# Attention on one core: TensorE's order laid out anew, the maxima split on GpSimd and copied on ScalarE, value products in a burst of three and one

## What is computed

```python
qkv = (x @ Wqkv).reshape(b, t, 3, H, hd).transpose(2, 0, 3, 1, 4)
q, k, v = (qkv[0], qkv[1], qkv[2])
scores = jnp.einsum('bhqd,bhkd->bhqk', q, k) * hd ** (-0.5)
scores = jnp.where(causal, scores, -jnp.inf)
attn = jax.nn.softmax(scores, axis=-1)
out = jnp.einsum('bhqk,bhkd->bhqd', attn, v)
return out.transpose(0, 2, 1, 3).reshape(b, t, c) @ Wproj + bproj
```

## Time and profile before

| what | before |
|---|---|
| median of three runs | 268.45 us (267.53 to 268.66) |
| profiled execution, its own time | 269.36 us |
| its span, first to last instruction | 267.5 us |
| mean granted TensorE clock | 0.852 of full speed |
| busy: VectorE (DVE) | 186.9 us, 70% |
| busy: TensorE (PE) | 161.9 us, 61% |
| busy: ScalarE (ACT) | 148.7 us, 56% |
| busy: GpSimd (POOL) | 74.6 us, 28% |

### The profile page before, as it was taken

One profiled execution on the slowest core, in us unless ns is written; L12 is line 12 of the kernel. 1 busy time (PEld: TensorE's weight loads), 2 busy tenths in 40 slices (PEclk: granted clock), 3 DMA queues, 4 the chain that ended last, 5 costly groups with the idle time before them and its releaser, 6 DMA issues.

```text
span 267.5 us, 4246 instructions
## 1 busy us (share of the span) xinstructions
PE 161.9 (61%) x1515; PEld 100.7 (38%) x1519; DVE 186.9 (70%) x523; ACT 148.7 (56%) x327; POOL 74.6 (28%) x88
## 2 busy tenths in 40 slices
PE   0222136907523400731848967898998998796985
PEld 0102034606412300401733524645545544453754
DVE  0688787899996697597584578778878877623411
ACT  3455769367795526693415452455645654876431
POOL 6243612234304224296014973000000000003110
PEclk9999999965795555595777977599999999999999
DMA  6995000000000000000000340312000000000011
GB/s 184 400 430 219 1 0 0 0 0 4 0 0 1 0 0 0 0 1 0 2 0 27 98 96 20 60 40 29 2 2 4 2 4 2 3 3 1 2 39 39
DMA packets 4491, 11.50 MB, mean 43 GB/s; under 512 B 1267, under 2 KB 2644, under 8 KB 3828
## 3 DMA queue, kind: packets, MB, share of 16 engines
q1 hardware_dynamic: 3510, 10.04, 10.9%
q0 software_dynamic: 960, 1.19, 1.8%
HBM read 8.24 MB, written 0.52 MB: 33 GB/s over the span
## 4 chain that ended last, share of the span: by engine, by line
PE 39%; DVE 38%; ACT 8%; POOL 5%; issue 4%; DMA 4%; SPq 1%; DVEq 0%; ACTq 0%
DVE negmax L1201 8%; PE ps L1551 6%; PE ps L1356 5%; PE ps L1491 4%; POOL uh L445 4%; PE ps L1581 3%; PE ps L1587 3%; PE ps L1447 2%; DMA cw<-in_cond_w 2%; PE ps L1531 2%; PE ps L1438 2%; PE ps L1415 2%; DVE u L1009 2%; ACT xhat L653 2%; DVE fg L1051 2%
## 5 line engine op out<-in xcount | busy, mean ns | idle before, releaser
L1201 DVE TENSOR_REDUCE negmax<-ps 128x1 f32<-128x384 f32 (+3 forms) x96 | 52.8, 595 | 16.0 <-PE ps L1493 16.0
L743 ACT ACTIVATE PT<-ps 128x1024 f32<-128x1024 f32 x40 | 40.8, 1025 | 34.6 <-PE ps L1537 34.2
L378 POOL TENSOR_TENSOR rstd<-veps,mhalf 128x4 f32<-128x4 f32 x8 | 8.1, 1011 | 114.4 <-DVE veps L840 114.4
L1491 PE MATMUL ps<-KS,QS 48*128 48x128 bf16 (+3 forms) x128 | 33.3, 325 | 1.1 <-DVE negmax L1201 0.8
L1356 PE MATMUL ps<-k_f,u 128*128 128x128 f32 x40 | 10.0, 425 | 32.6 <-ACT u L643 21.8
L1531 PE MATMUL ps<-QS,KS 51*128 51x512 bf16 (+3 forms) x128 | 24.6, 315 | 0.8 <-DMA QS<-nmT 0.7
L1492 PE MATMUL ps<-k_b 64*128 64x128 bf16 x128 | 24.9, 230 | 0.0
L1551 PE MATMUL ps<-PT,V 128*9 128x512 f32 (+3 forms) x256 | 22.5, 434 | 1.9 <-ACT PT L743 1.2
L1493 PE MATMUL ps<-k_b 64*128 64x64 bf16 x128 | 22.1, 197 | 0.0
L1356 PEld LDWEIGHTS ps<-k_f,u 128*128 128x128 f32 x40 | 7.6, 220 | 34.5 <-DVE u L1009 26.5
L1491 PEld LDWEIGHTS ps<-KS,QS 48*128 48x128 bf16 x128 | 11.0, 96 | 19.5 <-DVE negmax L1201 14.9
(11 more groups left out here) (211 smaller groups left out, 453.0 us busy)
## 6 DMA issues: line engine op xcount, KB each, us to landing
w<-in_wa SPq DMA_DIRECT2D x2, 1152.0 KB, 10.6
lw<-in_l_w SPq DMA_DIRECT2D x1, 1280.0 KB
brow<-in_bcast_rows SPq DMA_DIRECT2D x1, 1152.0 KB, 15.7
mw<-in_main_w SPq DMA_DIRECT2D x1, 1024.0 KB, 13.5
KS<-part POOLq DMA_DIRECT2D x12, 64.0 KB, 3.4
QS<-part SPq DMA_DIRECT2D x12, 64.0 KB
cw<-in_cond_w SPq DMA_DIRECT2D x1, 576.0 KB, 5.7
xs<-in_x SPq DMA_DIRECT2D x1, 512.0 KB, 7.3
```

The lines of the kernel that those rows point to most:

```text
L378: return nc.gpsimd.tensor_tensor(r, v, mhalf[0:v.shape[0], 0:v.shape[-1]], ALU.pow)
L743: nc.scalar.activation(PT[n % 2][:, s, :], bank(2 * (use % 2), 2), ACT.Exp).then_inc(S["p_ready"], 1)
L1201: V.tensor_reduce(negmax[n % 2][:, qt, h0:h0 + nh], bank(S_BANKS[k % 3])[:, 0:nh * w].rearrange("p (h w) -> p h w", w=w), AX.X, ALU.max, n ...
L1491: T.matmul(dst, QS[b][rows, h, tok(qt)], KS[b][rows, h, 0:w], start=True, stop=False)
```

## The change

The four splitting instructions go from VectorE to GpSimd, with a semaphore between each two. The copy of the transposed maxima goes from VectorE to ScalarE and raises a semaphore of its own, `nm_copied`, for which SP's transfers and the next user of the bank wait. On TensorE the transposes of the maxima move from behind item 2 to behind item 3, the transposes of the old values right behind them, exponent slot 4 from item 4 to item 5, and the products of key tiles 0, 1 and 3 together behind item 6. ScalarE copies the products one iteration part earlier, between exponent slots 1 and 2.

```diff
+MAXIMA_AT = 3
...
-            if i == 2 and n >= 1:
+            if i == MAXIMA_AT and n >= 1:
                 order.append((n - 1, "maxima"))
...
-E_OLD = {1: 3, 4: 4}
+E_OLD = {1: 3, 5: 4}
 E_NEW = {7: 0, 9: 1, 11: 2}
-PV_AT = {5: 0, 6: 1, 7: 3, 10: 2}
+PV_AT = {6: (0, 1, 3), 10: (2,)}
...
-                sp.wait_ge(S["s_used"], NUMBER[n, "maxima"] + 1)
+                sp.wait_ge(S["nm_copied"], n + 1)
...
+            def split_maxima(n):
+
+                nm = negmax[n % 2][:, :, :].rearrange("p t (a h) -> p t a h", a=2)
+                left = nmrest[:, :, :].rearrange("p t (a h) -> p t a h", a=2)
+                pt = nmpart[n % 2]
+                pool.wait_ge(S["s_used"], len(S_ITEMS) * (n + 1))
+                nc.gpsimd.tensor_copy(pt[:, :, :, 0, :], nm).then_inc(S["nm_hi"], 1)
+                pool.wait_ge(S["nm_hi"], n + 1)
+                nc.gpsimd.tensor_tensor(left, nm, pt[:, :, :, 0, :], ALU.subtract).then_inc(S["nm_left"], 1)
+                pool.wait_ge(S["nm_left"], n + 1)
+                nc.gpsimd.tensor_copy(pt[:, :, :, 1, :], left).then_inc(S["nm_mid"], 1)
+                pool.wait_ge(S["nm_mid"], n + 1)
+                nc.gpsimd.tensor_tensor(pt[:, :, :, 2, :], left, pt[:, :, :, 1, :], ALU.subtract
+                                        ).then_inc(S["nm_ready"], 1)
+
+            for n in range(N_GROUPS):
+                split_maxima(n)
...
+            def copy_maxima(n):
+                k = NUMBER[n, "maxima"]
+                act.wait_ge(S["s_pe"], k + 1)
+                if n >= 2:
+                    act.wait_ge(nm_stacked[n % 2], 32 * (n // 2))
+                nc.scalar.activation(nmT[n % 2][:, :], bank(S_BANKS[k % 3])[0:3 * HG, 0:L // 2].bitcast(BF16), ACT.Copy
+                                     ).then_inc(S["nm_copied"], 1)
+
             for n in range(N_GROUPS + 3):
-                if n >= 3:
-                    act.wait_ge(S["pv_pe"], n - 2)
-                    if n >= 5:
-                        act.wait_ge(S["at_pe"], n - 4)
-                    nc.scalar.activation(pvs[(n - 3) % 2][:, :], bank(6), ACT.Copy).then_inc(S["pv_ready"], 1)
-                for lag, slots in ((2, (3, 4)), (1, (0, 1, 2))):
-                    if 0 <= n - lag < N_GROUPS:
-                        for s in slots:
-                            exp_slot(n - lag, s)
-                            if n == N_GROUPS and s == 0:
-                                columns_of_attention(0)
+                if 2 <= n <= N_GROUPS + 1:
+                    exp_slot(n - 2, 3)
+                if 1 <= n <= N_GROUPS:
+                    copy_maxima(n - 1)
+                if 2 <= n <= N_GROUPS + 1:
+                    exp_slot(n - 2, 4)
+                if 1 <= n <= N_GROUPS:
+                    exp_slot(n - 1, 0)
+                    if n == N_GROUPS:
+                        columns_of_attention(0)
+                    exp_slot(n - 1, 1)
+                if 2 <= n <= N_GROUPS + 1:
+                    copy_values(n - 2)
+                if 1 <= n <= N_GROUPS:
+                    exp_slot(n - 1, 2)
...
+                if n >= 2 and i == 0:
+                    dve.wait_ge(S["nm_ready"], n - 1)
                 dve.wait_ge(S["s_pe"], k + 1)
                 V.tensor_reduce(negmax[n % 2][:, qt, h0:h0 + nh],
...
-                    if i == 2 and 1 <= n <= N_GROUPS:
-                        copy_maxima(n - 1)
...
-                if n < N_GROUPS:
-                    split_maxima(n)
...
+            def bank_free(k):
+
+                if k >= 3 and USES[k - 3][1] == "maxima":
+                    pe.wait_ge(S["nm_copied"], USES[k - 3][0] + 1)
+                elif k >= 3:
+                    pe.wait_ge(S["s_used"], SCORES[k - 3])
...
-                    if i == 2 and 1 <= n <= N_GROUPS:
+                    if i == MAXIMA_AT and 1 <= n <= N_GROUPS:
                         maxima(n - 1)
+                    if i == MAXIMA_AT and n >= 3:
+                        values_rows(n - 3)
                     if i in E_OLD and 2 <= n <= N_GROUPS + 1:
                         exp_slot(n - 2, E_OLD[i])
                     if i in E_NEW and 1 <= n <= N_GROUPS:
                         exp_slot(n - 1, E_NEW[i])
-                    if i == 3 and n >= 3:
-                        values_rows(n - 3)
                     if i in PV_AT and 2 <= n <= N_GROUPS + 1:
-                        values(n - 2, PV_AT[i])
+                        for kt in PV_AT[i]:
+                            values(n - 2, kt)
```

More of the change, by code:

```diff
@@ L104, in _rotation @@
                 order.append((n, i))
-            if i == 2 and n >= 1:
+            if i == MAXIMA_AT and n >= 1:
                 order.append((n - 1, "maxima"))
-    return {what: k for k, what in enumerate(order)}
-NUMBER = _rotation()
+    return order
+USES = _rotation()
+NUMBER = {what: k for k, what in enumerate(USES)}
+SCORES = [sum(i != "maxima" for _, i in USES[:k + 1]) for k in range(len(USES))]
 S_BANKS = (4, 5, 7)
@@ L744, in exp_slot, with copy_values @@
                                      ).then_inc(S["p_ready"], 1)
[L746 to L757 removed]
+            def copy_values(n):
+                act.wait_ge(S["pv_pe"], n + 1)
+                if n >= 2:
+                    act.wait_ge(S["at_pe"], n - 1)
+                nc.scalar.activation(pvs[n % 2][:, :], bank(6), ACT.Copy).then_inc(S["pv_ready"], 1)
+            def copy_maxima(n):
+                k = NUMBER[n, "maxima"]
+                act.wait_ge(S["s_pe"], k + 1)
+                if n >= 2:
+                    act.wait_ge(nm_stacked[n % 2], 32 * (n // 2))
+                nc.scalar.activation(nmT[n % 2][:, :], bank(S_BANKS[k % 3])[0:3 * HG, 0:L // 2].bitcast(BF16), ACT.Copy
+                                     ).then_inc(S["nm_copied"], 1)
+            for n in range(N_GROUPS + 3):
+                if 2 <= n <= N_GROUPS + 1:
[13 more added lines that the diff above has]
+                    exp_slot(n - 1, 2)
             modulate_columns(0, 1)
@@ L1203, in row_maxima @@
                                 AX.X, ALU.max, negate=True).then_inc(S["s_used"], 1)
[L1205 to L1223, removed]
             def divide(n):
@@ L1478, in score_item @@
                 w = (qt + 1) * P
-                if k >= 3:
-                    pe.wait_ge(S["s_used"], k - 2)
+                bank_free(k)
                 if i == 0 and n < PICKED:
@@ L1607, in _ @@
                         exp_slot(n - 1, E_NEW[i])
-                    if i == 3 and n >= 3:
-                        values_rows(n - 3)
                     if i in PV_AT and 2 <= n <= N_GROUPS + 1:
-                        values(n - 2, PV_AT[i])
+                        for kt in PV_AT[i]:
+                            values(n - 2, kt)
                     if n == N_GROUPS and i == 7:
-                        pe.wait_ge(S["s_used"], NUMBER[N_GROUPS - 1, "maxima"] + 1)
+                        pe.wait_ge(S["nm_copied"], N_GROUPS)
                         columns_of_attention(0)
```

2 lines of the change are left out of this document (1 added, 1 removed).

## The result

The changed kernel takes 261.72 us in the median of four runs (260.8 to 262.79); the kernel before, on the same chip, 268.56 (267.53 to 269.57). The ratio is 0.9741, with an interval of 0.9695 to 0.9786: 6.8 us less. The profiled execution took 261.13 us, with a span of 259.3 and a mean granted clock of 0.841.

A forecast was written before the change was run, and what follows sets the result against it. The prediction took a VectorE piece followed by a TensorE piece as the 9.74 us cycle's bound. Five cycles at -1.00, -0.5 before them and +0.4 at the end gave -5.1: a median of 263.4 us, range 261.0 to 268.6.

The forecast's parts named there:

- cheaper rival: Whole kernel: the split on GpSimd costs less, TensorE's cycle of 8.6 us stops further gain; 262.2 us, chance 0.17.
- T: Attention cycle: time from the end of the last wide maximum to the start of TensorE's transposes, forecast 1.37 us.
- The ring: Attention cycle, 9.74 us: one VectorE piece of 3.7 us plus one TensorE piece of 6.0 us, one after the other.
- slower rival: GpSimd's split, between last wide maximum and transposes: 0.56 us an instruction makes it late; 273.3 us, chance 0.13.
- rule of twice VectorE's time: GpSimd's split: as a rival, 0.36 us an instruction against VectorE's 0.18; 266.9 us, chance 0.14.
- Items 4 to 6 with slot 4: TensorE between value transposes and burst: 0.73 plus 0.35 us, with VectorE's division just covered.
- Item 7 with slot 0: TensorE behind the burst: 0.53 us to items 8 and 9, then 0.51 to VectorE's wide maxima.
- The floor of 8.6: TensorE's cycle less idle time and saved turns: 8.6 us, so no split below 1.23 us gains more.
- The copy on ScalarE: Transposed maxima: copy of 0.59 us, transfer landing at 7.57 against slot 0 at 7.93, so 0.36 to spare.
- The sum: Whole kernel: five steady cycles -5.0 us, the two before them -0.5, the end +0.4; together -5.1.
- signs of being right: Profile after: cycles of 8.6 to 9.0 us, no VectorE gap before next group, transposes waiting for GpSimd, its instructions 0.2 to 0.3.
- signs of being wrong: Profile after: GpSimd instructions over 0.4 us, slot 0 waiting for the transfer, or VectorE idle over 0.5 beside the burst.

The follow-up runs named there:

- split_alone: The kernel before, with only the four splitting instructions moved from VectorE to GpSimd: 269.38 us, ratio to before 1.0041.
- one_cast_more: The changed kernel, with GpSimd's first cast made twice, one after the other: 263.82 us.
- copy_on_vector: The changed kernel, with the copy of the transposed maxima back on VectorE, ahead of the division: 261.26 us.
- two_parts: The changed kernel, with the maxima split into two bf16 parts instead of three, two GpSimd instructions instead of four: 259.85 us.
- no_split: The changed kernel without the split: VectorE writes each maximum as bf16 at once, the other two parts zero: 258.80 us.
- burst_undone: The changed kernel, with the products back in four places, at items 5, 6, 7 and 10: 266.02 us.
- tile3_behind_slot0: The changed kernel, with the product of key tile 3 taken out of the burst and put behind exponent slot 0: 265.40 us.

## Why the prediction was right, and where its sizes were off

The sign and the mechanism held: 261.72 was measured, 263.4 predicted, in a range of 261.0 to 268.6. The time is nearer to the cheaper rival's 262.2, but that rival asked for a T below 1.23, which did not come. It stands only 0.7 above the lower end of the range. By the prediction's own steps:

- **What bounds.** The ring of one VectorE piece and one TensorE piece is shown by three runs: taking VectorE's share away without the order gave nothing (split_alone), one small instruction more on GpSimd showed almost in full (one_cast_more), and work put on VectorE off the ring did not show at all (copy_on_vector).
- **The split, T = 1.37.** Measured 1.27 (205.56, where the last wide maximum ends, to 206.83). The four instructions are 0.20 to 0.22, not 0.25; the line through 512 and 128 columns had given 0.22. The wait from the last one's end to the transposes is 0.15, not 0.05. The slower rival, with 0.56 each, took its price from the power and was far off. Nor was 0.56 the most that the trace had for small arithmetic on GpSimd, as the prediction says: the same power takes 1.03 on four columns.
- **The rule of twice VectorE's time** (the Trainium skill, GPSIMD Engine Reference, section Performance versus the Vector engine). This case's trace shows it at 512 columns but not at 16: 0.20 to 0.22 on GpSimd against 0.18 on VectorE.
- **The transposes wait for GpSimd alone; no gap on VectorE.** Both as said: 0.32 of idle time ended by GpSimd, nine maxima in a row.
- **Transposes and value transposes**, 0.34 and 0.59: measured 0.31 and 0.59.
- **Items 4 to 6 with slot 4, 0.73 + 0.35 = 1.08:** measured 1.00 (207.73 to 208.73). The division, held to be just covered, ended at 208.42, 0.3 ahead of the burst: covered.
- **The burst, 1.84:** measured 1.84 (208.73 to 210.57).
- **Item 7 with slot 0, 0.53, and 0.51 to VectorE.** With T it is the step most mis-sized: together 0.93 (210.57 to 211.50) instead of 1.04. The step took 0.99 from the kernel before and subtracted the product (0.34) and the turn (0.12), as if the instructions ran one after the other. Without a product between them, item 7, slot 0 and item 8 run partly side by side: item 7 to item 8 took 0.33. With 0.51 behind it the wide maxima could start at 211.41; they start at 211.50, because VectorE's maximum of item 7, which the prediction had off the ring, stands in front of them.
- **The cycle.** 0.10 (T) + 0.03 (transposes) + 0.08 (items 4 to 6) + 0.11 (item 7 to the wide maxima) = 0.32, so 8.74 becomes 8.42, which was measured.
- **The floor of 8.6** in the cheaper rival was too high for the same reason, and it made the lower end of the range narrower than it should have been: two_parts and no_split run at 8.06. It had counted the turns and the idle time, but not the score work that the products keep apart.
- **The copy on ScalarE.** Its duration held (0.59 taken, 0.586 measured in the row below), and slot 0 in the cycle did not wait for the transfer. But the cover was mis-read: the prediction put slot 0 0.23 behind item 7 and found 0.36 to spare, while slot 0 starts 0.01 behind item 7, in the kernel before (216.95 and 216.94) as in the changed one (210.58 and 210.57). From the copy's end to slot 0 are 2.74, against 2.69 for a slot that waits: what is to spare is about 0.05. As a gain it was nothing, which the sum had right: it credited the copy's 0.42 to VectorE's load, not to the cycle.

The group of the copy in the changed kernel (busy, mean ns of one, idle time ahead), and the copy in the timeline of the cycle:

```profile
L777 ACT ACTIVATE nmT<-ps 12x512 bf16<-12x512 bf16 x8 | 4.7, 586 | 3.8 <-PE ps L1525 3.5
```

```profile
207.25 0.59 ACT L777 ACTIVATE nmT<-ps 12x512 bf16<-12x512 bf16 x1
```

- **The sum.** Five steady cycles: -6.59 instead of -5.0. The two ahead of them: -0.24 instead of -0.5. The end: +0.07 instead of +0.4; the transposes come 0.28 later behind the wide maxima and the transfer lands 0.16 later, as forecast (0.4 and 0.2), but from slot 0 to the last four products are 6.49 instead of 6.83, so 0.34 came back and not 0.2. Together -6.76 instead of -5.1, which is the whole difference of 1.7 in the median.
- **The signs.** One of the signs of being right did not come: the steady cycle is 8.42, below the 8.6 to 9.0 that was named, for the four reasons in the sum of the cycle. And one of the signs of being wrong came although the prediction held: VectorE stands still for 1.22 beside the burst. It had been named as a sign that VectorE was held up there by something new. But its idle time in a cycle is 1.59 in all, and was 1.87 before; it is two gaps in the place of several. A sign of this kind should have been a statement on the ring (the wide maxima start late), and not on how an engine's idle time is spread.

## What to carry to other kernels

Find the ring first: write down which two or three waits pass the work round, and price an edit only by what it takes from that ring; a unit relieved off it gives nothing, and a wait taken away alone is followed by the next one at almost the same place. A move to another engine pays only if the waiting engine's order gives it something to do meanwhile, so change both together and test them apart. When durations are taken from a timeline where two kinds of matmul alternate, what they cost apart is not what they cost side by side: price both layouts, and take the side-by-side one for the lower end of the range.

## What was not expected of the hardware

- **Score items and exponent slots overtake each other on TensorE.** Each of their matmuls takes one half of the array's rows (`half_rows` in the code), and in the changed kernel item 8 started 0.15 and 0.18 ahead of masks that stand before it in the program. The Trainium skill says in TensorE: Matmul & The Clock Gate, Part 3, that matmuls start and end strictly in program order; the starts in this trace do not agree, and the measurement decides.
- **A product between them ends it.** A matmul over all 128 rows (the products, the transposes) waits for both and holds both back: the same item 7 to item 8 took 0.33 without and 0.99 with a product of 0.34 in between. The Trainium skill, TensorEngine Tiling (Array Packing), section Key Properties, says that a change of the tiling mode drains the engine; the 0.32 left here agrees.
- **The granted clock after an idle stretch.** In split_alone TensorE stood still for 1.43 ahead of the last transposes, and the granted clock was 0.83 in the ten us from 229, so for a part of them at the lower level of 1.2 GHz: 16 products took 3.18 instead of 1.69. The kernel before stood still for 1.15 at this place and kept 1.00. But the longer idle time alone is not the cause: burst_undone and tile3_behind_slot0 stood still for 1.43 there as well, one_cast_more for 1.55, and all three kept 1.00. What else decided in split_alone is not shown; these are single profiled executions. The place in burst_undone:

```profile
226.76 0.38 PE L1525 MATMUL ps<-k_b,nmpart 128*12 128x128 bf16 x4 [1.43 <-POOL nmpart L480]
...
228.49 1.69 PE L1573 MATMUL ps<-PT,V 128*9 128x512 f32 x16 [0.27 <-DVE attn L1251]
```
